# Split fp32r products for three of the six blocks of a down projection

## The chip, the cores and the metric

One core of one Trainium2 chip runs the whole kernel. The metric is the device time in microseconds of one execution, the median of several runs. All times below are of the kernel before the change.

## What is computed

A layer with three residual parts on x of 32 x 32 tokens of 512 numbers (1024 tokens): a cross attention, a gated delta-rule attention, and a mixture of 8 experts, of which each token takes two. The change touches the experts alone:

```python
probs = jax.nn.softmax(scores, axis=-1)
routing_weights, routing_idx = jax.lax.top_k(probs, TOP_K)          # TOP_K = 2 of 8
gate = jnp.einsum('bted,edf->btef', dispatched, gate_proj)           # D = 512, F = 1408
up = jnp.einsum('bted,edf->btef', dispatched, up_proj)
acts = jax.nn.silu(gate) * up
expert_out = jnp.einsum('btef,efd->bted', acts, down_proj)
```

## The kernel before

The kernel sorts the 2 x 1024 token copies by expert into 23 tiles of 128 slots (TILES). The function experts runs them one after the other. A tile's 1408 hidden columns are cut into NB = 6 blocks: five of 256 and one of 128. STEPS = 138 counts the blocks of all tiles, n is the running number, s the tile, b the block in it. Expert weights lie in w_gu (gate and up) and w_d (down); the SP queue loads them for the next tile in three groups each, only where the expert changes (cond=fresh), each group once the last block that used it is done.

Gate and up are computed in "three fp32r products": the activations and the weights are each split into a high part in the narrower type fp32r and a low part (the difference), and hi x hi, hi x lo and lo x hi are added up in PSUM. ScalarE casts the high part of a weight block (gh, L1697), VectorE subtracts to get the low part (gl, L1758), in a ring of four buffers, about three blocks ahead. The activations of a tile are split once (xh L1679, xl L1749).

TensorE's loop does, at each n: gate_up(n) (L1629 to L1631, 12 products), down(n-2) (L1652, two chunks of 128 rows, one for the half block, each an fp32 matmul that the chip runs as two instructions), turn_h(n-1) (L1639, two transposes), and in block 4 turn_x of the next tile (L1616). Between them ScalarE computes silu (L1709), VectorE the product with up (hid, L1791), and ScalarE copies the turned block out of PSUM (hT, L1720).

ScalarE's order at each n is: silu(n), store_y of the tile that ended two blocks ago (L1685 and a DMA from its queue), split_gate_up(n+3), the copy of hT(n-1), and in block 4 take_x. VectorE's is: hid(n), split_gate_up(n+2), in block 4 split_x; once, at n = 24, places() (L1767 to L1773), and in the last blocks gather_sum. GpSimd gathers the rows of y (L1741) once all but the last tile are stored, and VectorE adds them to x_nat (L1778); the last tile's y comes by matmuls (L1673, L1805). Each engine runs its instructions in order, and every hand-over is a semaphore.

Of the kernel before, what the change touches and what calls it, by code (L numbers as in the profile page):

```python
# [11 lines left out]
F32 = mybir.dt.float32  # L12
F32R = mybir.dt.float32r
U8 = mybir.dt.uint8
I32 = mybir.dt.int32
ALU = mybir.AluOpType
# [3 lines left out]
P = 128  # L20
B, N, C = 32, 32, 512
TOK = B * N
NT = TOK // P
# [20 lines left out]
BLK = 256  # L44
RING = 4
NB = -(-F // BLK)
# [1475 lines left out]
def experts(nc, d, ps, ident, x_nat, xn3, slot, slot_f, slot_w, tile_expert, column, hot, scattered, w_gu, w_d, gu_in, d_in, out):  # L1522

    with ExitStack() as ctx:
        sb = lambda name, shape, dt=F32: ctx.enter_context(nc.sbuf_tensor(name, shape, dt))
        sem = lambda name: ctx.enter_context(nc.semaphore(name))
# [2 lines left out]
        gh, gl = ([sb(f"{name}{i}", [P, KC, 2, BLK], F32R) for i in range(RING)] for name in ("gh", "gl"))  # L1532
        silu = [sb(f"silu{i}", [P, BLK]) for i in range(2)]
        hid = [sb(f"hid{i}", [P, BLK]) for i in range(2)]
        hT = [sb(f"hT{i}", [P, BLK // P, P]) for i in range(2)]
        y = [sb(f"y{i}", [P, C]) for i in range(2)]
        yg = [[xn3[:, 2 * (t % (NT // 2)) + r, :] for t in range(NT)] for r in range(2)]
        place, placeT, hot2 = hot, sb("placeT", [P, NT, P]), sb("place2", [P, NT, P])
        rel = sb("rel", [P, 2, NT])
        place_done, p_turned, p_copied, added, f_done, f_added, own = (  # L1540
            sem("place_done"), sem("p_turned"), sem("p_copied"), sem("t_added"), sem("f_done"), sem("f_added"), sem("e_own"))
# [6 lines left out]
        GU_BANK, H_BANK, X_BANK, Y_BANK = 0, 3, 5, 6  # L1548
        STEPS = TILES * NB
# [4 lines left out]
        with nc.Block() as block:  # L1554
# [39 lines left out]
            @block.tensor  # L1594
            def _(pe):
                def pick_first():
                    for k in range(KC):
                        for t in range(NT):
                            mm = pe.matmul(ps[X_BANK][:, k * P:(k + 1) * P], xn3[:, t, k * P:(k + 1) * P], hot[:, t, :],  # L1599
                                           start=(t == 0), stop=(t == NT - 1))  # L1600
                    mm.then_inc(x_turned, 1)

                def turn_places(x):
                    pe.wait_ge(place_done, 1)
                    pe.wait_ge(xl_done, TILES)
                    if x:
                        pe.wait_ge(p_copied, x)
                    for t in range(4):
                        mm = pe.transpose(ps[X_BANK][:, t * P:(t + 1) * P], place[:, 4 * x + t, :], ident[:, :])
                    mm.then_inc(p_turned, 1)  # L1610

                def turn_x(s):
                    pe.wait_ge(x_in[s % 3], 16 * (s // 3 + (s % 3 > 0)))
                    pe.wait_ge(xl_done, s)
                    for k in range(KC):
                        mm = pe.transpose(ps[X_BANK][:, k * P:(k + 1) * P], xs[s % 3][:, k * P:(k + 1) * P], ident[:, :])  # L1616
                    mm.then_inc(x_turned, 1)

                def gate_up(n):
                    s, b, bw = n // NB, n % NB, width(n % NB)  # L1620
                    if b == 0:
                        pe.wait_ge(xl_done, s + 1)
                    pe.wait_ge(gl_done, n + 1)
                    if n >= 3:
                        pe.wait_ge(hid_done, n - 2)
                    bank = ps[GU_BANK + n % 3][:, 0:2 * bw].rearrange("p (a f) -> p a f", a=2)
                    for k in range(KC):
                        hi, lo = gh[n % RING][:, k, :, 0:bw], gl[n % RING][:, k, :, 0:bw]
                        pe.matmul(bank, xh[s % 2][:, k, :], hi, start=(k == 0), stop=False)  # L1629
                        pe.matmul(bank, xh[s % 2][:, k, :], lo, start=False, stop=False)  # L1630
                        mm = pe.matmul(bank, xl[s % 2][:, k, :], hi, start=False, stop=(k == KC - 1))  # L1631
                    mm.then_inc(gu_done, 1)

                def turn_h(n):
                    pe.wait_ge(hid_done, n + 1)
                    if n >= 2:
                        pe.wait_ge(hT_done, n - 1)
                    for c in range(width(n % NB) // P):
                        mm = pe.transpose(ps[H_BANK + n % 2][:, c * P:(c + 1) * P], hid[n % 2][:, c * P:(c + 1) * P], ident[:, :])  # L1639
                    mm.then_inc(h_turned, 1)  # L1640

                def down(n):
                    s, b = n // NB, n % NB
                    pe.wait_ge(hT_done, n + 1)
                    if b % 2 == 0:
                        pe.wait_ge(d_in[b // 2], 16 * (s + 1))
                    if b == 0 and s >= 2:
                        pe.wait_ge(y_ready, s - 1)
                    cs = range(width(b) // P)
                    bank = ps[Y_BANK + s % 2]  # L1650
                    for c in cs:
                        mm = pe.matmul(bank, hT[n % 2][:, c, :], w_d[:, b * (BLK // P) + c, :], start=(b == 0 and c == 0),  # L1652
                                       stop=(b == NB - 1 and c == cs[-1]))
                    mm.then_inc(d_done, 1)

                pick_first()
                for n in range(STEPS + 2):
                    if n < STEPS:
                        gate_up(n)
                    if n >= 2:  # L1660
                        down(n - 2)
                    if 1 <= n <= STEPS:
                        turn_h(n - 1)
                    if n % NB == TURN_AT and n // NB + 1 < TILES:
                        turn_x(n // NB + 1)
                    if n in (STEPS - 4, STEPS - 2):
                        turn_places((n - STEPS + 4) // 2)
                pe.wait_ge(y_ready, TILES)
                pe.wait_ge(p_copied, 2)
                for t in range(NT):  # L1670
                    if t >= 6:
                        pe.wait_ge(f_added, t - 5)
                    pe.matmul(ps[t % 6], placeT[:, t, :], y[(TILES - 1) % 2][:, :], start=True, stop=True).then_inc(f_done, 1)  # L1673

            @block.scalar
            def _(act):
# [14 lines left out]
                def split_gate_up(n):  # L1691
# [3 lines left out]
                    if n >= RING:  # L1695
                        act.wait_ge(gu_done, n - RING + 1)
                    nc.scalar.copy(gh[n % RING][:, :, :, 0:bw].rearrange("p k a f -> p (k a) f"),  # L1697
                                   w_gu[:, :, :, b * BLK:b * BLK + bw].rearrange("p k a f -> p (k a) f")).then_inc(gh_done, 1)

                for n in range(3):  # L1700
                    split_gate_up(n)
                take_x(0)
                for n in range(STEPS + 2):
                    if n < STEPS:
                        bw = width(n % NB)
                        act.wait_ge(gu_done, n + 1)
                        if n >= 2:
                            act.wait_ge(hid_done, n - 1)
                        nc.scalar.activation(silu[n % 2][:, 0:bw], ps[GU_BANK + n % 3][:, 0:bw], ACT.Silu).then_inc(silu_done, 1)  # L1709
                    if n >= 2 and (n - 2) % NB == NB - 1:  # L1710
                        store_y((n - 2) // NB)
                    if n + 3 < STEPS:
                        split_gate_up(n + 3)
                    if 1 <= n <= STEPS:
                        m = n - 1
                        bw = width(m % NB)
                        act.wait_ge(h_turned, m + 1)
                        if m >= 2:
                            act.wait_ge(d_done, m - 1)
                        nc.scalar.copy(hT[m % 2][:, 0:bw // P, :].rearrange("p c n -> p (c n)"),  # L1720
                                       ps[H_BANK + m % 2][:, 0:bw]).then_inc(hT_done, 1)
                    if n % NB == TURN_AT and n // NB + 1 < TILES:
                        take_x(n // NB + 1)
                    if n in (STEPS - 3, STEPS - 1):
                        x = (n - STEPS + 3) // 2
                        act.wait_ge(p_turned, x + 1)
                        nc.scalar.copy(placeT[:, 4 * x:4 * x + 4, :].rearrange("p t n -> p (t n)"), ps[X_BANK]).then_inc(p_copied, 1)
# [18 lines left out]
            def _(dve):  # L1746
# [6 lines left out]
                def split_gate_up(n):  # L1753
                    b, bw = n % NB, width(n % NB)
                    dve.wait_ge(gh_done, n + 1)
                    if n >= RING:
# [3 lines left out]
                                            gh[n % RING][:, :, :, 0:bw].rearrange("p k a f -> p (k a) f").bitcast(F32),  # L1760
                                            ALU.subtract).then_inc(gl_done, 1)

                link = Chain(dve, own).link

                def places():
# [19 lines left out]
                for n in range(STEPS + 1):  # L1785
                    if n < STEPS:
                        bw = width(n % NB)
                        dve.wait_ge(silu_done, n + 1)
                        if n >= 2:
                            dve.wait_ge(h_turned, n - 1)  # L1790
                        nc.vector.tensor_tensor(hid[n % 2][:, 0:bw], silu[n % 2][:, 0:bw], ps[GU_BANK + n % 3][:, bw:2 * bw],  # L1791
                                                ALU.mult).then_inc(hid_done, 1)
                    if 0 < n < STEPS - 2:
                        split_gate_up(n + 2)
                    if n % NB == TURN_AT and n // NB + 1 < TILES:
# [81 lines left out]
```

## Time and profile before

| | |
|---|---|
| median of 3 runs | 1874.05 us (1873.61 to 1875.43) |
| the profiled execution | 1869.62 us, span of the trace 1867.5 us |
| TensorE busy over the span | 1538.5 us (82%) |
| VectorE | 1199.0 us (64%) |
| ScalarE | 713.3 us (38%) |
| the expert stage | from about 1220 us to the end |
| down matmuls L1652 | 506 instructions, 242.2 us busy |
| gh casts L1697, gl subtractions L1758 | 138 each, 242.0 and 290.5 us |

An execution of the kernel is followed by the profiler; the span is from its first to its last instruction. Busy times of TensorE's matmuls overlap each other, so how long a group of them takes is read from the start of one to the start of the next.

### The profile page before, as it was taken

To read this page: it belongs to the slowest core of one execution; us is meant where nothing else is said; L and a number is where in the kernel's file an instruction comes from. 1 tells how busy PE (TensorE), PEld (TensorE's weight loads), DVE (VectorE), ACT (ScalarE), POOL (GpSimd) and SP (SyncE) were. 2 spreads that over 40 slices of the span, in tenths; PEclk is the share of its full clock that TensorE was granted. 3 is DMA by queue.
4 is the path that set the end of the run, shared out by engine and by line. 5 is a ranking of instruction groups with operands and counts; after the bars stand their busy time and mean duration, and the time that the engine had idled before them with its cause. 6 is when DMAs were issued, how large, how long until landed. Compare 5 with 4: busy or idle time off the path is not lost. (4 is left out here: it accounts for less than half of the span.)

```text
span 1867.5 us, 22300 instructions
## 1 busy us (share of the span) xinstructions
PE 1538.5 (82%) x7255; PEld 1144.2 (61%) x7255; DVE 1199.0 (64%) x2644; ACT 713.3 (38%) x1364; POOL 96.1 (5%) x261
## 2 busy tenths in 40 slices
PE   6999999999799999349100089489999999999998
PEld 3888888888667767213000088466666666666664
DVE  4366555665336786999999756455655555556555
ACT  2343343333355455201000222155555555555552
POOL 0000000000000000022112100130000000000003
PEclk9999999999899999779555579689999999999999
DMA  3211011100241441450100231525605514426004
GB/s 119 80 35 33 18 34 34 34 24 10 95 66 44 81 80 41 70 180 1 45 0 0 69 83 36 192 96 209 208 18 203 208 56 165 160 72 207 13 17 141
DMA packets 134201, 152.94 MB, mean 82 GB/s; under 512 B 64096, under 2 KB 84960, under 8 KB 134112
## 3 DMA queue, kind: packets, MB, share of 16 engines
q1 hardware_dynamic: 128384, 137.68, 24.4%
q0 software_dynamic: 2560, 8.39, 1.4%
q10 hardware_dynamic: 3168, 5.77, 0.8%
q8 instruction: 45, 0.74, 0.2%
q14 instruction: 44, 0.36, 0.1%
HBM read 250.25 MB, written 31.33 MB: 151 GB/s over the span
## 5 line engine op out<-in xcount | busy, mean ns | idle before, releaser
L1758 DVE TENSOR_TENSOR gl<-w_gu,gh 128x2048 fp32r<-128x2048 f32 x138 | 290.5, 2106 | 6.8 <-ACT gh L1697 6.7
L1697 ACT CAST gh<-w_gu 128x2048 fp32r<-128x2048 f32 x138 | 242.0, 1755 | 41.8 <-PEq L1413 19.2
L1652 PE MATMUL bank<-w_d,hT 128*128 128x512 f32 x506 | 242.2, 597 | 8.8 <-ACT hT L1720 8.0
L1791 DVE TENSOR_TENSOR hid<-silu,bank 128x256 f32<-128x256 f32 x138 | 55.0, 399 | 264.6 <-ACT silu L1709 264.6
L1629 PE MATMUL bank<-gh,xh 128*128 128x512 f32 (+1 forms) x552 | 217.7, 394 | 1.7 <-DVE xl L1749 1.4
L1631 PE MATMUL bank<-gh,xl 128*128 128x512 f32 (+1 forms) x552 | 205.9, 373 | 0.0
L1630 PE MATMUL bank<-gl,xh 128*128 128x512 f32 (+1 forms) x552 | 205.5, 372 | 0.0
L1229 PE MATMUL bank<-o_v,xnT 128*128 128x64 f32 x256 | 36.1, 310 | 177.9 <-DMA o_v<-scratch_v_rows 177.9
L1229 PEld LDWEIGHTS bank<-o_v,xnT 128*128 128x128 f32 x256 | 35.8, 227 | 178.7 <-DMA o_v<-scratch_v_rows 178.7
L1652 PEld LDWEIGHTS bank<-w_d,hT 128*128 128x128 f32 x506 | 91.7, 189 | 82.0 <-issue 56.9
L1709 ACT ACTIVATE silu<-bank 128x256 f32<-128x256 f32 x138 | 50.6, 367 | 218.3 <-PE bank L1631 216.3
L539 DVE COPY probT<-bank 128x512 f32<-128x512 f32 x64 | 41.1, 683 | 127.9 <-PE bank L421 127.9
L1629 PEld LDWEIGHTS bank<-gh,xh 128*128 128x128 f32 x552 | 104.0, 188 | 22.7 <-issue 6.4
L1631 PEld LDWEIGHTS bank<-gh,xl 128*128 128x128 f32 x552 | 103.8, 188 | 19.3
L1630 PEld LDWEIGHTS bank<-gl,xh 128*128 128x128 f32 x552 | 104.3, 189 | 14.6
L1064 ACT ACTIVATE r_root<-r_nm 128x8 f32<-128x8 f32 x32 | 6.7, 208 | 275.2 <-DVE r_nm L1142 275.2
L1056 PE MATMUL bank<-w_kg,xnT 128*128 128x512 f32 x128 | 60.8, 619 | 52.8 <-DMA bg_row<-in_bg 52.8
L486 ACT ACTIVATE prob<-bank,neg_max 128x257 f32<-128x257 f32 x128 | 59.1, 474 | 74.1 <-DVE neg_max L521 74.1
L1112 DVE TENSOR_TENSOR r_prod<-r_gram,r_pr 128x512 f32<-128x512 f32 (+23 forms) x158 | 83.6, 547 | 0.0
L370 PE MATMUL bank<-xa_wkv_hi,ctx_hi 128*128 128x512 f32 x192 | 78.9, 411 | 0.6 <-PEq L280 0.6
L1056 PEld LDWEIGHTS bank<-w_kg,xnT 128*128 128x128 f32 x128 | 23.6, 195 | 88.4 <-DMA bg_row<-in_bg 53.0
L1639 PEld LDWEIGHTS bank<-ident,hid 128*128 128x128 f32 x253 | 35.4, 140 | 65.9 <-issue 49.8
(296 smaller groups left out, 3097.1 us busy)
## 6 DMA issues: line engine op xcount, KB each, us to landing
w_gu<-in_gate_proj SPq DMA_DIRECT2D x46, 1024.0 KB
w_gu<-in_up_proj SPq DMA_DIRECT2D x46, 1024.0 KB
w_d<-in_down_proj SPq DMA_DIRECT2D x46, 1024.0 KB
w_gu<-in_gate_proj SPq DMA_DIRECT2D x23, 768.0 KB
w_gu<-in_up_proj SPq DMA_DIRECT2D x23, 768.0 KB
w_d<-in_down_proj SPq DMA_DIRECT2D x23, 768.0 KB
ctx_raw<-in_ctxT SPq DMA_DIRECT2D x32, 385.5 KB, 3.7
scratch_x_slots<-r_outw SPq DMA_DIRECT2D x1, 5888.0 KB, 19.3
```

The source lines that it names most:

```text
L370: pe.matmul(bank, hi(k), other_hi(k), start=(k == 0), stop=False)
L486: nc.scalar.activation(prob[s][:, c, :], ps[c][:, 0:M], ACT.Exp, bias=neg_max[s][:, c:c + 1], accum_out=total[s][:, c:c + 1]).then_inc(exp ...
L1056: pe.matmul(ps[n % 8], xnT[:, k, t * P:(t + 1) * P], wg[:, k, hf * 512:(hf + 1) * 512], start=(k == 0), stop=False)
L1112: ins = tt(parts[x][:, a], G[:, :, lo:hi, 2, 0:cols], bc(pr[nxt % 2][:, a, :, None, 0:cols], [SG, hi - lo, cols]), ALU.mult)
L1229: mm = pe.matmul(ps[O_BANK + 2 * s + h // 8][:, (h % 8) * DK:(h % 8 + 1) * DK], outw[s][:, h, :], v_row[s][:, h, :], start=True, stop=True)
L1629: pe.matmul(bank, xh[s % 2][:, k, :], hi, start=(k == 0), stop=False)
L1630: pe.matmul(bank, xh[s % 2][:, k, :], lo, start=False, stop=False)
L1631: mm = pe.matmul(bank, xl[s % 2][:, k, :], hi, start=False, stop=(k == KC - 1))
L1652: mm = pe.matmul(bank, hT[n % 2][:, c, :], w_d[:, b * (BLK // P) + c, :], start=(b == 0 and c == 0), stop=(b == NB - 1 and c == cs[-1]))
L1697: nc.scalar.copy(gh[n % RING][:, :, :, 0:bw].rearrange("p k a f -> p (k a) f"), w_gu[:, :, :, b * BLK:b * BLK + bw].rearrange("p k a f -> ...
L1758: nc.vector.tensor_tensor(gl[n % RING][:, :, :, 0:bw].rearrange("p k a f -> p (k a) f"), w_gu[:, :, :, b * BLK:b * BLK + bw].rearrange("p ...
L1791: nc.vector.tensor_tensor(hid[n % 2][:, 0:bw], silu[n % 2][:, 0:bw], ps[GU_BANK + n % 3][:, bw:2 * bw], ALU.mult).then_inc(hid_done, 1)
```

## The change

In blocks 0, 2 and 4 of each tile down() takes three fp32r products for each chunk, in blocks 1, 3 and 5 it stays with one fp32 matmul. For the changed blocks ScalarE casts dh, the high part of w_d's block, and VectorE subtracts dl; the turned hidden block is copied as fp32r (hh), and VectorE subtracts hl from PSUM. dh, dl, hh and hl are single buffers. On ScalarE the copy of the hidden block moves: in even n it stands behind the gate and up cast and before the new cast, in odd n directly behind silu, ahead of store_y and of the gate and up cast. The buffer place2 gives way to placeT.

```diff
-        hT = [sb(f"hT{i}", [P, BLK // P, P]) for i in range(2)]
+        hh, hl = sb("hh", [P, BLK // P, P], F32R), sb("hl", [P, BLK // P, P], F32R)
+        hT = [hh, sb("hT", [P, BLK // P, P])]
+        dh, dl = sb("dh", [P, BLK // P, C], F32R), sb("dl", [P, BLK // P, C], F32R)
...
                     if n >= 2:
                         pe.wait_ge(hT_done, n - 1)
+                        if n % 2 == 0:
+                            pe.wait_ge(hl_done, n // 2)
...
-                    for c in cs:
-                        mm = pe.matmul(bank, hT[n % 2][:, c, :], w_d[:, b * (BLK // P) + c, :], start=(b == 0 and c == 0),
-                                       stop=(b == NB - 1 and c == cs[-1]))
+                    if b % 2 == 0:
+                        pe.wait_ge(dl_done, n // 2 + 1)
+                        pe.wait_ge(hl_done, n // 2 + 1)
+                        for c in cs:
+                            pe.matmul(bank, hh[:, c, :], dh[:, c, :], start=(b == 0 and c == 0), stop=False)
+                            pe.matmul(bank, hh[:, c, :], dl[:, c, :], start=False, stop=False)
+                            mm = pe.matmul(bank, hl[:, c, :], dh[:, c, :], start=False, stop=False)
+                    else:
+                        for c in cs:
+                            mm = pe.matmul(bank, hT[1][:, c, :], w_d[:, b * (BLK // P) + c, :], start=False,
+                                           stop=(b == NB - 1 and c == cs[-1]))
...
+                def take_hidden(n):
+                    bw = width(n % NB)
+                    act.wait_ge(h_turned, n + 1)
+                    if n >= 2:
+                        act.wait_ge(d_done, n - 1)
+                    nc.scalar.copy(hT[n % 2][:, 0:bw // P, :].rearrange("p c n -> p (c n)"),
+                                   ps[H_BANK + n % 2][:, 0:bw]).then_inc(hT_done, 1)
+
+                def split_down(n):
+                    s, b = n // NB, n % NB
+                    act.wait_ge(d_in[b // 2], 16 * (s + 1))
+                    if n >= 2:
+                        act.wait_ge(d_done, n - 1)
+                    nc.scalar.copy(dh[:, :, :], w_d[:, b * (BLK // P):(b + 1) * (BLK // P), :]).then_inc(dh_done, 1)
...
+                    if n % 2 == 0 and n + 3 < STEPS:
+                        split_gate_up(n + 3)
+                    if 1 <= n <= STEPS:
+                        take_hidden(n - 1)
+                    if n % 2 == 0 and n < STEPS:
+                        split_down(n)
                     if n >= 2 and (n - 2) % NB == NB - 1:
                         store_y((n - 2) // NB)
-                    if n + 3 < STEPS:
+                    if n % 2 and n + 3 < STEPS:
                         split_gate_up(n + 3)
-                    if 1 <= n <= STEPS:
...
+                def split_down(n):
+                    b = n % NB
+                    dve.wait_ge(dh_done, n // 2 + 1)
+                    nc.vector.tensor_tensor(dl[:, :, :], w_d[:, b * (BLK // P):(b + 1) * (BLK // P), :], dh[:, :, :].bitcast(F32),
+                                            ALU.subtract).then_inc(dl_done, 1)
+                    dve.wait_ge(hT_done, n + 1)
+                    nc.vector.tensor_tensor(hl[:, :, :].rearrange("p c n -> p (c n)"), ps[H_BANK][:, 0:BLK],
+                                            hh[:, :, :].rearrange("p c n -> p (c n)").bitcast(F32), ALU.subtract).then_inc(hl_done, 1)
...
+                    if n % 2 and n < STEPS:
+                        split_down(n - 1)
                     if 0 < n < STEPS - 2:
                         split_gate_up(n + 2)
```

## Rows read from the trace of the kernel before

**Rows 1.** Stretch view: us, busy us and count of each engine, PEclk, DMA share, GB/s.

```profile
1224.00:1860.00 636.00, 623.06 (x2573) 424.99 (x2572) 365.41 (x334) 341.44 (x462) 29.58 (x25) 1.00 0.36 125
```

**Rows 2.** Waits of TensorE, 1225 to 1845 us: who waited for whom, total, times, longest.

```profile
PE bank L1652 <- ACT hT L1720: 8.0, 24, 0.4
```

**Rows 3.** Timeline of TensorE: start, duration, instruction, count, idle time before it.

```profile
1293.71 1.98 PE L1652 MATMUL bank<-w_d,hT 128*128 128x512 f32 x4 [0.34 <-ACT hT L1720]
...
1301.14 0.39 PE L1629 MATMUL bank<-gh,xh 128*128 128x512 f32 x1
...
1303.18 1.88 PE L1652 MATMUL bank<-w_d,hT 128*128 128x512 f32 x4
1304.89 0.38 PE L1639 MATMUL bank<-ident,hid 128*128 128x128 f32 x2
...
1305.47 0.36 PE L1629 MATMUL bank<-gh,xh 128*128 128x256 f32 x1
...
1306.98 1.88 PE L1652 MATMUL bank<-w_d,hT 128*128 128x512 f32 x4
1308.69 0.38 PE L1639 MATMUL bank<-ident,hid 128*128 128x128 f32 x2
1308.83 0.48 PE L1629 MATMUL bank<-gh,xh 128*128 128x512 f32 x1
...
1311.65 1.88 PE L1652 MATMUL bank<-w_d,hT 128*128 128x512 f32 x4
...
1320.58 1.98 PE L1652 MATMUL bank<-w_d,hT 128*128 128x512 f32 x4 [0.34 <-ACT hT L1720]
```

**Rows 4.** The same view in the output projection, ahead of the experts.

```profile
1126.05 0.39 PE L1253 MATMUL bank<-wo_hi,o_gT_hi 128*128 128x512 f32 x1
...
1130.83 1.04 PE L1239 MATMUL bank<-ident,r_gram 128*128 128x128 f32 x8
```

**Rows 5.** Timeline of TensorE's weight loads, inside an fp32 down block.

```profile
1303.61 0.19 PEld L1652 LDWEIGHTS bank<-w_d,hT 128*128 128x128 f32 x1 [0.24 <-issue]
```

**Rows 6.** Groups by form: total busy us, mean ns, idle time before them.

```profile
L1697 ACT CAST gh<-w_gu 128x1024 fp32r<-128x1024 f32 x23 | 24.0, 1044 | 0.0
L1758 DVE TENSOR_TENSOR gl<-w_gu,gh 128x1024 fp32r<-128x1024 f32 x23 | 28.0, 1218 | 0.0
```

**Rows 7.** Timeline of ScalarE, columns as in rows 3.

```profile
1273.96 1.91 ACT L1697 CAST gh<-w_gu 128x2048 fp32r<-128x2048 f32 x1 [2.20 <-DMA w_gu<-in_up_proj]
...
1303.38 0.38 ACT L1709 ACTIVATE silu<-bank 128x256 f32<-128x256 f32 x1 [2.23 <-PE bank L1631]
1303.66 1.89 ACT L1697 CAST gh<-w_gu 128x2048 fp32r<-128x2048 f32 x1
1305.45 0.38 ACT L1720 COPY hT<-bank 128x256 f32<-128x256 f32 x1
1305.75 0.59 ACT L1679 CAST xh<-bank 128x512 fp32r<-128x512 f32 x1
```

**Rows 8.** Timeline of VectorE.

```profile
1303.79 0.42 DVE L1791 TENSOR_TENSOR hid<-silu,bank 128x256 f32<-128x256 f32 x1 [3.12 <-ACT silu L1709]
1304.13 2.28 DVE L1758 TENSOR_TENSOR gl<-w_gu,gh 128x2048 fp32r<-128x2048 f32 x1
1306.37 0.69 DVE L1749 TENSOR_TENSOR xl<-bank,xh 128x512 fp32r<-128x512 f32 x1
...
1341.68 0.17 DVE L1767 TENSOR_SCALAR rel<-slot_f 128x16 f32<-128x16 f32 x1
...
1347.26 0.41 DVE L1791 TENSOR_TENSOR hid<-silu,bank 128x256 f32<-128x256 f32 x1
```

**Rows 9.** SP queue's first load of a burst, and the stretch after it (columns of rows 1).

```profile
1265.19 0.40 SPq L1568 DMA_DIRECT2D w_gu<-in_gate_proj  x1
...
1288.00:1290.00 2.00, 2.00 (x9) 1.45 (x8) 0.02 (x2) 0.39 (x1) 0.00 (x0) 1.00 0.06 20
```

**Rows 10.** Timeline of GpSimd: the first gather of y.

```profile
1832.55 0.98 POOL L1741 DMA_INDIRECT xn<-scratch_y_slots,slot  x1 [594.96 <-DMA scratch_y_slots<-y]
```

More of the change, by code:

```diff
@@ L1534, in experts @@
         hid = [sb(f"hid{i}", [P, BLK]) for i in range(2)]
-        hT = [sb(f"hT{i}", [P, BLK // P, P]) for i in range(2)]
+        hh, hl = sb("hh", [P, BLK // P, P], F32R), sb("hl", [P, BLK // P, P], F32R)
+        hT = [hh, sb("hT", [P, BLK // P, P])]
+        dh, dl = sb("dh", [P, BLK // P, C], F32R), sb("dl", [P, BLK // P, C], F32R)
+        hl_done, dh_done, dl_done = sem("hl_done"), sem("dh_done"), sem("dl_done")
         y = [sb(f"y{i}", [P, C]) for i in range(2)]
         yg = [[xn3[:, 2 * (t % (NT // 2)) + r, :] for t in range(NT)] for r in range(2)]
-        place, placeT, hot2 = hot, sb("placeT", [P, NT, P]), sb("place2", [P, NT, P])
+        place, placeT = hot, sb("placeT", [P, NT, P])
+        hot2 = placeT
         rel = sb("rel", [P, 2, NT])
@@ L1709, in _ @@
                         nc.scalar.activation(silu[n % 2][:, 0:bw], ps[GU_BANK + n % 3][:, 0:bw], ACT.Silu).then_inc(silu_done, 1)
+                    if n % 2 == 0 and n + 3 < STEPS:
[4 more added lines that the diff above has]
+                        split_down(n)
                     if n >= 2 and (n - 2) % NB == NB - 1:
                         store_y((n - 2) // NB)
-                    if n + 3 < STEPS:
+                    if n % 2 and n + 3 < STEPS:
                         split_gate_up(n + 3)
-                    if 1 <= n <= STEPS:
[L1715 to L1721, printed above, removed]
                     if n % NB == TURN_AT and n // NB + 1 < TILES:
```

## The prediction

> **What bounds the kernel now.** The page gives means over stages with different limits, so I cut out the expert stage with a stretch view [rows 1]: from 1224 to 1860 us TensorE is busy 623.1 of 636 us at clock 1.00, the weight loads (PEld) 425, VectorE 365, ScalarE 341. TensorE sets the time there, and ScalarE and VectorE have over 40% of theirs free. The waits of TensorE say the same [rows 2]: 8.0 us in 24 waits for hT, a third of a microsecond each, and next to nothing else. Then I read one tile instruction by instruction [rows 3]. A tile has six blocks (0 to 5, the last half as wide), and one turn of TensorE's loop is gate_up(n), down(n-2), turn_h(n-1). The tile's period is 26.87 us, from the hT wait in block 2 at 1293.71 to the one at 1320.58.
>
> **The products themselves.** Busy times on a pipelined TensorE overlap, so I take start to start. The four fp32 matmul instructions of a down block start at 1306.98 and the turn behind them at 1308.69: 1.71 us [rows 3]. Nine fp32r products of 128x512 in gate_up take from 1301.14 to 1303.18, 0.227 us each [rows 3]. The output projection has the same shape of product as the changed one (activations turned and split as weights, 512 columns of a split matrix) in threes of the same order: 21 of them from 1126.05 to 1130.83, 0.228 us [rows 4]. A changed block has two chunks of three products: 6 x 0.227 = 1.36 us. Gain 0.35 us a block. There are 3 x 23 = 69 such blocks; the end of the kernel hangs on the store of tile 21 (below), before which 66 have run: 66 x 0.35 = **23.1 us**. Bounds: 0.43 a block, 28 us, if a product went at half of an fp32 instruction (1.71 / 4 / 2 = 0.214); and 0.25, 16 us, if each group also paid the 0.10 us that an fp32 group pays behind a wait (1.98 for four against 1.88). I take the pace between them, since gate_up and the projection both show it.
>
> The fp32 rows leave the weight loader 0.24 us idle before a load of 0.19 us [rows 5]; at 0.227 us a product such a load still fits beside the product ahead. The Trainium skill (TensorE: Matmul & The Clock Gate, Back-to-back issue gap) gives N/2.4 + 2.5 ns warm, 216 ns for 512 columns; by it the six products would take 1.30 us and the sum would gain some 4 us more. The rows of this case show 227 ns, and they decide.
>
> **The order on ScalarE.** Now hT is copied behind the cast of gate and up (gh), which in block 1 starts late because the store of y goes first. That is TensorE's 0.33 us wait in each tile [rows 2, 3]. The change puts take_hidden right behind silu in odd steps, the store of y and the gh cast behind it. hT of block 0 then comes as soon as it is turned, over 2 us ahead of its use. 23 of the 24 waits go (the last lies behind the store of tile 21): 23 x 0.33 = **7.7 us**. Bound: nothing, if hl, which now ends that chain, is just as late.
>
> **What is added elsewhere.** Per changed block ScalarE casts dh 128x1024, 1.04 us like the half gh, VectorE subtracts dl 128x1024, 1.22 us like the half gl [rows 6], and hl from PSUM, 128x256, 0.42 us like hid [rows 8]. Per tile that is 3.1 us on ScalarE and 4.9 on VectorE. Start to start (each overlaps the next a little) VectorE's tile is 5 gl x 2.24, one 1.18, hid 1.9, xl 0.65, dl 3.5, hl 1.0: 19.5 us, in a new period of 26.87 - 0.33 - 3 x 0.35 = 25.5. ScalarE has about 17.6. Both fit on average; whether they fit in their order has to be walked.
>
> The walk counts from the end of gate_up(4) on TensorE, with latencies of the rows: silu starts 0.2 behind the end and hid 0.61 (1303.18, 1303.38, 1303.79), gh follows silu 0.28 later and takes 1.79, hT 0.30, xh 0.60, hid to gl 0.34 [rows 3, 7, 8]; a whole gate_up is 2.82, the half one 1.51, turn_h 0.14, with turn_x 0.58 [rows 3]; hT starts 0.42 behind the turn's start (estimate: the turn's 0.38 and a hand-over). ScalarE: silu 0.2, gh to 2.3, hT(3) to 2.6, dh(4) to 3.5, xh to 4.1. TensorE: down(2) 1.36, turns 0.58, gate_up(5) 1.51, end at 3.45; down(3) in fp32 1.71, turn 0.14, so gate_up(0) of the next tile may start at 5.3. It needs xl: VectorE has it at 4.8. Margin 0.5. silu(5) is 0.4 late behind xh, hid(5) is done at 5.0, dl(4) at 6.2, hl(4) at 6.5, gl(1) at 8.8. gate_up(0) ends at 8.1 and down(4) needs hl(4) there: margin 1.6. down(4) and the short turn end at 9.5, where gate_up(1) needs gl(1): margin 0.7. hid(0) 9.1, gl(2) 11.3; gate_up(1) ends at 12.3; hid(1), dl(0), hl(0) to 14.8, needed at 16.15: margin 1.3; gl(3) at 17.1, needed at 17.65: margin 0.6. An ordinary odd step has 1.7 for hl and 1.0 for gl. So there is no wait in the steady tile, though three margins are only 0.5 to 0.7. The wait that turn_h gains (hl_done) is for hl of two blocks before, long past. What queues behind a waiting hl on VectorE is gl of three blocks ahead, and it is in the walk.
>
> **Where the cover is gone.** (a) places(), once, in block 0 of tile 4, holds VectorE from 1341.68 to 1347.26, 5.6 us [rows 8]. In the walk that moves hl(0) to 18.8 against 16.15 and gl(3) to 21.1 against 17.65: **+3.4 us** (bounds 1 to 5.6). (b) The first tile starts with an empty pipe, and the same count puts hl(0), then gl(3), behind: **+0.7** (estimate from the same rows; 0 to 2). (c) Where the expert changes (7 times by ScalarE's waits for w_gu), gh waits for the load: 2.20 us at 1273.96 [rows 7], 8.8 us from its issue [rows 9]. By the walk gh(0) is 0.7 to 1.4 us late and xh with it, so gate_up(0) waits up to 0.3: **+1** for all seven (0 to 5). The dh cast needs w_d two blocks earlier than the matmul did. The burst of loads issued from 1265.19 has ended by 1288 [rows 9], and dh(0), carried over to the new clock, comes at 1285.6; w_d's first part is not the burst's last, so I take nothing. (d) The tail. The gathers on GpSimd start when the y of tile 21 has landed (1832.55) [rows 10], and they, the sums and the last additions make the end; TensorE's last blocks lie beside that path. The y copy now has take_hidden ahead of it: +0.5. The gathers wait for VectorE's sums, which in the last tile stand behind dl and hl: +0.3. Together **+0.8**. w_d's loads keep their place in the SP queue; GpSimd's queue and the stages before 1224 us are untouched.
>
> **Sum.** -23.1 - 7.7 + 3.4 + 0.7 + 1.0 + 0.8 = -24.9 us. The profiled execution took 1869.62 us (span 1867.5), so 1844.7 for a like one. The median of the runs is 1874.05, 4.4 above it: **1849**.
>
> **Rivals.**
> 1. A thin margin fails in each tile: the three places of 0.5 to 0.7 us are late by 0.5 us a tile in all, 22 x 0.5 = 11, so 1860. For it: the walk is good to 0.1 or 0.2 us a step only, and it has many. Against: gl takes the same 2.28 with a gh at its side (1304.13) as any other [rows 7, 8], so the engines don't slow each other. 0.13.
> 2. Slower: VectorE's line sets the period. hl(4), blocked on hT(4), keeps gl(1), and TensorE waits at every start of a tile. It decides once the stretch of 8.8 us up to gl(1) grows past 9.5; to eat the whole 25 us and 8 more, 1.5 a tile, it must grow to 11.0, by a quarter, for instance by hT coming a step later than I read. Then 1849 + 22 x 1.5 = 1882. Against it are the equal durations just named. 0.06.
> 3. The products' gain doesn't come: six weight loads replace four, and if the two more were exposed they would cost 2 x 0.19 = 0.38 us a block against the 0.35 gained. Only the hT waits go, less the small terms: 1849 + 66 x 0.38 = 1874, no change. Trace Analysis of the Trainium skill (Identifying the Most-Contended Engine) judges TensorE's headroom by the busy share of its weight loads, which this change raises. Here that share is 67% [rows 1]; 69 x 2 loads of 0.19 more, 26 us, leave it under 75%, so by itself the rule doesn't bind. The rows at 0.227 speak against exposed loads. 0.06.
> 4. The hT waits stay, as hl waits: 1857. It lies within the range. 0.06.
>
> **How the numbers follow.** The forecast holds 0.69; its own range is 1842 (all 69 blocks, and no price for a, b and c) to 1854 (b and c at their upper bounds). With rivals 4 and 1 the range is 1842 to 1862. Under 1842 I leave 0.06 in the forecast's share, over 1862 some 0.12. A measurement of this kernel tells about 0.2% (3.7 us) from no change. Faster by more than that: 0.87; within it: 0.06 (rival 3); slower: 0.07 (rival 2 and a rest).
>
> **What would show it.** After: six products of a changed block start to start in 1.36 us; a tile period of 25.5 us and no TensorE wait for hT in block 2; ScalarE near 66% and VectorE near 76% busy in a plain stretch; one gap of some 3 us behind places(), for hl and gl; y of tile 21 some 25 us earlier, and the stretch from it to the end unchanged within 1 us. Waits for xl or gl once a tile would be rival 1, a period over 26.9 rival 2, 1.7 us for six products rival 3. What would make me wrong most simply is an engine's order that I walked wrongly at the turn from one tile to the next.

## The result and the profile after

The changed kernel takes 1846.45 us (median of 4, 1845.26 to 1846.84) against 1873.98 in the same session: ratio 0.9842, 95% interval 0.9824 to 0.9861 (the quotient of the two medians is 0.9853, inside it). Forecast were 1849, in 1842 to 1862. Its profiled execution took 1845.26 us (span 1843.2), so profile against profile it is 24.4 us shorter, where the sum said 24.9.

The busy line of the profile's page (engine, busy us, share of the span, instructions) and the stretch view for two whole tiles (columns of [rows 1]):

```profile
PE 1516.0 (82%) x7393; PEld 1175.5 (64%) x7393; DVE 1300.7 (71%) x2782; ACT 778.1 (42%) x1433; POOL 97.1 (5%) x261
```

```profile
1436.94:1462.15 25.21, 25.21 (x117) 19.32 (x116) 19.40 (x20) 17.48 (x24) 0.00 (x0) 1.00 0.46 163
1462.15:1487.36 25.21, 25.21 (x118) 19.32 (x117) 19.75 (x20) 17.93 (x24) 0.00 (x0) 1.00 0.64 223
```

In a plain tile TensorE is busy all the time at clock 1.00, VectorE 77 to 78%, ScalarE 69 to 71% and the weight loads 77%. TensorE's timeline (columns of [rows 3]), a changed block, the turn of tiles, and one place where the expert changes:

```profile
1303.09 0.39 PE L1662 MATMUL bank<-dh,hh 128*128 128x512 f32 x1
...
1304.45 0.38 PE L1646 MATMUL bank<-ident,hid 128*128 128x128 f32 x2
...
1308.39 0.48 PE L1634 MATMUL bank<-gh,xh 128*128 128x512 f32 x1
...
1312.60 0.47 PE L1634 MATMUL bank<-gh,xh 128*128 128x512 f32 x1
...
1320.79 0.47 PE L1634 MATMUL bank<-gh,xh 128*128 128x512 f32 x1
...
1332.18 1.99 PE L1667 MATMUL bank<-w_d,hT 128*128 128x512 f32 x4 [0.28 <-ACT hT L1720]
...
1436.94 0.60 PE L1621 MATMUL bank<-ident,xs 128*128 128x128 f32 x4
1462.15 0.60 PE L1621 MATMUL bank<-ident,xs 128*128 128x128 f32 x4
```

Six products take from 1303.09 to 1304.45, 1.36 us, where four fp32 instructions took 1.71 [rows 3]. The turn of x at 1436.94 and at 1462.15 gives the period: 25.21 us, where it was 26.87. Of the 21 periods between the first and the last turn of x, 17 are 25.21 within 0.01; the others are taken up below. TensorE's waits, 1220 to 1860 us (who waited for whom, total, times, longest):

```profile
PE bank L1688 <- DVE x_nat L1844: 5.1, 1, 5.1
PE bank L1662 <- DVE hl L1797: 3.7, 2, 2.7
PE bank L1667 <- ACT hT L1720: 1.8, 5, 0.6
...
PE bank L1634 <- DVE gl L1786: 0.3, 1, 0.3
```

The 8.0 us in 24 waits for hT [rows 2] are now 1.8 in 5. Of the two waits for hl one, 2.7 us, lies behind places(); the other, 1.0, in the last tile, beside the path that ends the kernel, as does one of the five for hT (0.35).

The wait behind places() cost more than itself. TensorE around it, and the stretch view of three pieces of it (the number behind POOL is the granted clock):

```profile
1342.47 0.48 PE L1634 MATMUL bank<-gh,xh 128*128 128x512 f32 x1
...
1348.20 0.47 PE L1662 MATMUL bank<-dh,hh 128*128 128x512 f32 x1 [2.73 <-DVE hl L1797]
...
1350.31 0.80 PE L1634 MATMUL bank<-gh,xh 128*128 128x512 f32 x1
...
1354.36 1.88 PE L1667 MATMUL bank<-w_d,hT 128*128 128x512 f32 x4
```

```profile
1348.00:1349.00 1.00, 0.80 (x4) 0.69 (x5) 1.00 (x2) 0.00 (x0) 0.00 (x0) 1.00 0.67 256
1351.00:1352.00 1.00, 1.00 (x4) 0.81 (x3) 1.00 (x1) 0.80 (x1) 0.00 (x0) 0.50 0.03 8
1353.00:1354.00 1.00, 1.00 (x6) 0.83 (x5) 0.00 (x0) 0.00 (x0) 0.00 (x0) 1.00 0.00 0
```

From 1342.47 to 1354.36 are 11.89 us; the same instructions one tile earlier took 7.18 (1316.44 to 1323.62), so 4.7 us are lost. The down block starts 2.9 late, and gate_up(3) at 1350.31 starts 3.5 late, 0.06 behind the end of the gl(3) that it needs (1350.25). The last 1.2 us are lost behind that, since the granted clock had fallen from 1.00 to 0.50 (2.4 to 1.2 GHz): from 1349.43 to 1352.61 products go at about 0.43 us instead of 0.227. In the kernel before, where TensorE waited 0.28 us at this place, the clock stayed at 1.00.

VectorE around the same turn of tiles:

```profile
1307.20 0.69 DVE L1777 TENSOR_TENSOR xl<-bank,xh 128x512 fp32r<-128x512 f32 x1 [0.87 <-ACT xh L1694]
...
1309.47 2.28 DVE L1786 TENSOR_TENSOR gl<-w_gu,gh 128x2048 fp32r<-128x2048 f32 x1
...
1317.87 2.28 DVE L1786 TENSOR_TENSOR gl<-w_gu,gh 128x2048 fp32r<-128x2048 f32 x1
```

xl is ready at 1307.89 and gate_up(0) starts at 1308.39: margin 0.5, as walked. gl(1) ends at 1311.75, 0.85 before 1312.60 (walked 0.7). gl(3) ends at 1320.15, 0.64 before 1320.79 (walked 0.6).

Where the 24.4 us lie, from the two profiled executions (starts of the first matmul behind the routing, of the first and the last gather of y, and the span's end):

| stretch | before | after | difference | by the sum |
|---|---|---|---|---|
| up to the first matmul of the experts | 1220.57 | 1223.14 | +2.6 | 0 |
| to the first gather of y [rows 10] | 611.98 | 583.58 | -28.4 | -25.2 |
| first to last gather | 21.62 | 23.07 | +1.5 | +0.3 |
| to the end | 13.33 | 13.41 | +0.1 | 0 |

So the total agrees better than its parts, and that is luck: the expert stage gained 3.2 us more than forecast, the tail lost 1.2 more, and 2.6 came in ahead of everything that was changed. That last part is no effect of the change: in another execution of the same changed kernel (below) the experts start at 1220.58.

### The profile page after: what moved, and what is told of

Same layout as the page of the kernel before. It is cut to its first block and busy times, and to the rows that moved or that the text cites. A ratio compares the mean times of both kernels' runs of the same rounds, so it can differ in the third digit from the quotient of the medians.

```text
span 1843.2 us, 22920 instructions
## 1 busy us (share of the span) xinstructions
PE 1516.0 (82%) x7393; PEld 1175.5 (64%) x7393; DVE 1300.7 (71%) x2782; ACT 778.1 (42%) x1433; POOL 97.1 (5%) x261
## 3 DMA queue, kind: packets, MB, share of 16 engines
q1 hardware_dynamic: 128384, 137.68, 24.4%
## 5 line engine op out<-in xcount | busy, mean ns | idle before, releaser
L1635 PEld LDWEIGHTS bank<-gl,xh 128*128 128x128 f32 x552 | 104.6, 189 | 14.6
L1667 PE MATMUL bank<-w_d,hT 128*128 128x512 f32 x230 | 110.4, 594 | 1.8 <-ACT hT L1720 1.8
L1794 DVE TENSOR_TENSOR dl<-w_d,dh 128x1024 fp32r<-128x1024 f32 x69 | 84.0, 1218 | 0.0
L481 ACT COPY xkT<-bank 128x512 f32<-128x512 f32 x64 | 37.6, 588 | 91.3 <-PE bank L372 91.3
```

The costliest lines, as they stand in the source:

```text
L1667: mm = pe.matmul(bank, hT[1][:, c, :], w_d[:, b * (BLK // P) + c, :], start=False, stop=(b == NB - 1 and c == cs[-1]))
L1794: nc.vector.tensor_tensor(dl[:, :, :], w_d[:, b * (BLK // P):(b + 1) * (BLK // P), :], dh[:, :, :].bitcast(F32), ALU.subtract).then_inc(dl ...
```

## Experiments

The sessions of the experiments had the kernel before at 1877.2 and 1877.5 us (1872.3 to 1884.4), a scatter of several us. Medians are therefore read by their ratio to the kernel before of their session, and small terms from the trace: the period of a plain tile (from turn to turn of x) and the stretch from the first matmul of the experts to the first gather. A ratio is compared with the changed kernel's 0.9842; 0.001 of it is 1.9 us. Two profiles of the changed kernel have 583.58 and 585.49 us for that stretch (the second waits 1.3 us longer for hT where the expert changes), so differences under 2 us in it say nothing alone; the waits then count. The kernel before has one profile only. Some diffs show only the main lines of an edit.

**1. Only the order.** The kernel before with ScalarE's copy of hT moved:

```diff
-                    if n >= 2 and (n - 2) % NB == NB - 1:
-                        store_y((n - 2) // NB)
-                    if n + 3 < STEPS:
+                    if n % 2 == 0 and n + 3 < STEPS:
                         split_gate_up(n + 3)
                     if 1 <= n <= STEPS:
                         m = n - 1
...
+                    if n >= 2 and (n - 2) % NB == NB - 1:
+                        store_y((n - 2) // NB)
+                    if n % 2 and n + 3 < STEPS:
+                        split_gate_up(n + 3)
```

> The kernel before with only ScalarE's order changed: the copy of the turned block stands ahead of store_y and of the gate and up cast in odd n, all products stay fp32. Theory A (a wait that the trace shows as 0.33 us of idle costs 0.60 us start to start, since the product ahead overlaps it and the group restarts cold): 23 waits x 0.60 less some 1 to 2 us of new waits where the expert changes, so about 1862. Theory B (the idle column is the whole cost): 23 x 0.33 less the same, about 1868.

Measured: 1860.01 us, ratio 0.9906 (0.9889 to 0.9922). TensorE's timeline and waits:

```profile
1439.25 0.60 PE L1616 MATMUL bank<-ident,xs 128*128 128x128 f32 x4
1465.51 0.60 PE L1616 MATMUL bank<-ident,xs 128*128 128x128 f32 x4
```

```profile
PE bank L1629 <- DVE gl L1760: 0.9, 1, 0.9
PE bank L1652 <- ACT hT L1718: 0.8, 2, 0.5
```

The period is 26.26 us: one wait that the idle column gives as 0.33 us was worth 26.87 - 26.26 = 0.61. Over 23 tiles that is 14 us; with the new waits and the later store of y the stretch to the first gather is 600.94 against 611.98, 11.0 less. By the ratio the kernel gained 17.6 us (14.6 to 20.8), where A had 12 and B (7.7 less the same) 6. Theory A holds, if anything too low; B does not.

**2. The products in the old order.**

```diff
+                    if n >= 2 and (n - 2) % NB == NB - 1:
+                        store_y((n - 2) // NB)
-                    if n % 2 == 0 and n + 3 < STEPS:
+                    if n + 3 < STEPS:
                         split_gate_up(n + 3)
                     if 1 <= n <= STEPS:
                         take_hidden(n - 1)
                     if n % 2 == 0 and n < STEPS:
                         split_down(n)
-                    if n >= 2 and (n - 2) % NB == NB - 1:
-                        store_y((n - 2) // NB)
-                    if n % 2 and n + 3 < STEPS:
-                        split_gate_up(n + 3)
```

> The changed kernel with ScalarE's old order: store_y, gate and up cast, then the copy of the turned block. Theory A (the order is a condition of the change): hl of block 0 comes about 1.1 us after TensorE needs it and gl of block 3 behind it about 0.7 us late, so about 40 us more than the changed kernel, 1880 to 1890, slower than before. Theory B (the order and the products are separate gains): only the old hT waits come back, 1846 + 14 = 1860.

Measured: 1878.53 us, ratio 1.0009 (0.9996 to 1.0022): no change clear of noise to the kernel before. Waits of TensorE, 1225 to 1845 us:

```profile
PE bank L1662 <- DVE hl L1795: 23.6, 26, 2.5
PE bank L1634 <- DVE gl L1784: 5.8, 22, 0.3
```

A wait for hl and then one for gl in each tile, as walked. The usual period is 26.87 us (12 of the 21 lie within 0.02 of it, the others above), 1.66 over the changed kernel's and the same as the kernel before's. To the first gather it is 31.9 us more than the changed kernel (615.47 against 583.58), by the ratios 31: short of A's 40, and twice B's 14. The order gains by itself too (experiment 1), but without it the products gain nothing: it is a condition of theirs.

**3. All splits made, no products.**

```diff
-                            pe.matmul(bank, hh[:, c, :], dh[:, c, :], start=(b == 0 and c == 0), stop=False)
-                            pe.matmul(bank, hh[:, c, :], dl[:, c, :], start=False, stop=False)
-                            mm = pe.matmul(bank, hl[:, c, :], dh[:, c, :], start=False, stop=False)
+                            mm = pe.matmul(bank, hh[:, c, :].bitcast(F32), w_d[:, b * (BLK // P) + c, :], start=(b == 0 and c == 0), stop=False)
```

> The changed kernel with all splits made and waited for, but the down blocks 0, 2 and 4 as one fp32 matmul a chunk on the rounded hidden values (the low part of the hidden values is left out of the result). Theory A (a block gains 0.35 us, the splits cost TensorE nothing in the steady tile): 66 x 0.35 = 23 above the changed kernel, 1869 to 1870. Theory B (the prediction's extra 3 us came from the products, 0.40 us a block): 1873. If the splits cost something in the steady tile, this kernel less the first one of this call is more than 8 us.

Measured: 1865.2 us, ratio 0.9931 (0.9906 to 0.9955). Against the changed kernel's 0.9842 that is 17 us by the ratios and 604.47 - 583.58 = 20.9 by the stretch (19.0 to the second profile), both under A's 23.

```profile
1444.40 0.60 PE L1621 MATMUL bank<-ident,xs 128*128 128x128 f32 x4
1470.65 0.60 PE L1621 MATMUL bank<-ident,xs 128*128 128x128 f32 x4
```

The period is 26.25 us. To experiment 1 that is 0.01: 8 us a tile of added work on ScalarE and VectorE cost TensorE nothing. To the changed kernel it is 1.04, three times 0.35. So a block gains what was forecast, and B's 0.40 is out. That the 20.9 are 2.2 us under the 66 x 0.35 fits the tiles in which the expert changes: by the periods the changed kernel loses 3.5 us there, this one 1.4. That the loads come later against a shorter tile is likely, but was not tried.

**4. 1.2 us more on VectorE, at two places.** dl of block 4 made twice, and in another kernel dl of block 2 (b == 2 in the line below):

```diff
                     dve.wait_ge(dh_done, n // 2 + 1)
+                    if b == 4:
+                        link(nc.vector.tensor_tensor(dl[:, :, :], w_d[:, b * (BLK // P):(b + 1) * (BLK // P), :], dh[:, :, :].bitcast(F32),
+                                                     ALU.subtract))
```

> The changed kernel with VectorE's subtraction for dl of block 4 done twice, 1.2 us more in each tile, where the walk leaves 0.7 to 0.85 us until gl(1) is needed. Theory A (the margin by the walk decides): 0.3 to 0.6 us a tile, 1853 to 1860. Theory B (VectorE's free quarter of the tile takes it up): 1846 to 1847.

> The same 1.2 us of extra VectorE work a tile, but for dl of block 2, where hl has 1.7 us until it is needed. Theory A (the place decides, not the amount): no change to the changed kernel, 1846 to 1847. Theory B (VectorE's total decides): the same cost as with block 4.

Measured: block 4 1858.89 us, ratio 0.9904 (0.9879 to 0.9929); block 2 1843.74 us, 0.9823 (0.9803 to 0.9843). Waits of TensorE, first with block 4, then with block 2:

```profile
PE bank L1634 <- DVE gl L1786: 6.2, 23, 0.4
PE bank L1662 <- DVE hl L1800: 4.8, 2, 3.2
```

```profile
PE bank L1662 <- DVE hl L1800: 3.8, 2, 2.8
PE bank L1667 <- ACT hT L1720: 3.1, 5, 1.3
```

The same work, 1.2 us a tile, costs 0.47 us a tile in the one place (period 25.68, from 1444.89 to 1470.57) and nothing in the other (25.21, from 1437.30 to 1462.51). VectorE is busy 81% of the first period and 82% of the second. The shift exceeds the margin by 1.2 less 0.85, that is 0.35; the rest is about what the restart of the group costs.

**5. The remaining waits.** places() cut into five parts in block 3 of tiles 4 to 8; the first gate and up load of the next tile issued ahead of the last down load of this one; and both, with the last eight matmuls in eight PSUM banks:

```diff
-                    if n == 4 * NB:
-                        places()
+                    if n % NB == 3 and 4 <= n // NB < 9:
+                        places(n // NB - 4)
```

```diff
                     load_down(s, e, 1, fresh)
+                    e2, fresh2 = expert(s + 1)
+                    load_x(s + 2)
+                    load_gate_up(s + 1, e2, 0, fresh2)
                     load_down(s, e, 2, fresh)
```

```diff
-                    if t >= 6:
-                        pe.wait_ge(f_added, t - 5)
-                    pe.matmul(ps[t % 6], placeT[:, t, :], ...)
+                    pe.matmul(ps[t], placeT[:, t, :], ...)
```

> The changed kernel with places() cut into five parts, in block 3 of tiles 4 to 8, where VectorE waits for silu. Theory A (its 2.7 us wait for hl and the restart are lost for good): 3 us less than the changed kernel, 1843.5. Theory B (TensorE catches it up later): no change.

> The changed kernel with the first gate and up load of the next tile issued ahead of the last down load of this one, some 3.7 us earlier. Theory A (the five waits for hT in block 5 where the expert changes come from the late load, 0.36 + 0.26 us each): 3 us less, 1843.5. Theory B (they come from ScalarE's fuller queue): no change. If w_d's last part comes late now, slower.

> Both of these, and the last eight matmuls into eight PSUM banks, so that none waits for VectorE. In the changed kernel the last one waits 5.1 us and then runs at clock 0.50, but VectorE's seven additions hide all but 0.3 us of it. Theory A: 3 + 3 + 0.4, so 1840. Theory B (the end hangs on the gathers alone, whose pace sets it, and gains before the store of tile 21 don't reach it in full): 1843 or more.

Measured: 1843.01 us (0.9818, 0.9801 to 0.9836), 1841.31 us (0.9812, 0.9791 to 0.9832), 1839.89 us (0.9799, 0.9778 to 0.982). The intervals overlap each other, and the first two that of the changed kernel, so the single steps are read from the trace; the third lies just under it. The stretch to the first gather is 581.15, 579.54 and 575.29 us, that is 2.4, 4.0 and 8.3 less than the changed kernel's 583.58. Waits of TensorE with places() spread, then with the early load, then together:

```profile
PE bank L1667 <- ACT hT L1720: 3.0, 5, 1.3
PE bank L1662 <- DVE hl L1797: 1.0, 1, 1.0
```

```profile
PE bank L1671 <- DVE hl L1806: 3.5, 2, 2.5
...
PE bank L1676 <- ACT hT L1729: 0.4, 1, 0.4
```

```profile
PE bank L1671 <- DVE hl L1804: 1.0, 1, 1.0
...
PE bank L1676 <- ACT hT L1727: 0.4, 1, 0.4
```

Each step takes away the waits that it was meant for: hl's 2.7 us at places(), and hT's where the expert changes (the 0.4 that stays is the one in the last tile). By the waits theory A of each holds. What they are worth is read from the periods. With both steps all 21 are 25.21 within 0.01; the changed kernel loses 8.2 us in four of them: 4.7 to places() and 3.5 where the expert changes (in each of the four; places() falls into one of them). With the early load alone the tile of places() still loses 4.3, and with places() spread the clock stays at 1.00 there. So places() costs 4 to 5 us and not the 3 of the expectation; the first step shows only 2.4 of it in the stretch, in part since this execution waits 2.7 us for hT where the expert changes, against 1.5 in the changed kernel. What the eight banks give was not measured by itself.

**6. The tail.** The last tile's down blocks in fp32, without dh, dl and hl, which TensorE's idle end can afford; the changed kernel again beside it; and everything together:

```diff
-                    if n % 2 and n < STEPS:
+                    if n % 2 and n < STEPS - NB:
                         split_down(n - 1)
```

> The changed kernel itself once more, so that the next two are compared with it in one session: 0.984 of the kernel before, as measured.

> The changed kernel with the last tile's down blocks all in fp32 and without its dh, dl and hl, since TensorE's last blocks lie beside the path that ends the kernel. Theory A (the 16 gathers of y take 23.1 us instead of 21.6 because VectorE's dl and hl run beside them): the stretch from the first to the last gather falls to 21.6, the time by 1.5 us. Theory B (the gathers' pace has another cause): no change within 0.3 us of that stretch.

> places() spread, the load ahead, eight banks and the last tile in fp32 together. Theory A of each: 8.3 us less than the changed kernel for the first three by the stretch up to the first gather, and 1.5 more at the end, so about 9 to 10 below it, 0.979 of the kernel before. If the last tile gives nothing: 8 below.

The diff is the line for VectorE; ScalarE and TensorE have the like. Measured in one session: the changed kernel 1845.04 us (0.9843, 0.982 to 0.9865), with the last tile in fp32 1843.61 (0.9831, 0.9809 to 0.9853), everything together 1835.64 (0.9784, 0.9763 to 0.9806). GpSimd's gathers (start, duration) in the changed kernel, VectorE beside them, and the gathers with the last tile in fp32:

```profile
1806.72 0.98 POOL L1769 DMA_INDIRECT xn<-scratch_y_slots,slot  x1 [566.55 <-DMA scratch_y_slots<-y]
1808.01 2.00 POOL L1769 DMA_INDIRECT xn<-scratch_y_slots,slot  x1 [0.31 <-issue]
...
1811.56 1.77 POOL L1769 DMA_INDIRECT xn<-scratch_y_slots,slot  x1 [0.30 <-issue]
1813.64 1.62 POOL L1769 DMA_INDIRECT xn<-scratch_y_slots,slot  x1 [0.30 <-issue]
...
1829.79 1.07 POOL L1769 DMA_INDIRECT xn<-scratch_y_slots,slot  x1 [0.30 <-issue]
```

```profile
1806.89 2.28 DVE L1786 TENSOR_TENSOR gl<-w_gu,gh 128x2048 fp32r<-128x2048 f32 x1
...
1811.30 1.22 DVE L1794 TENSOR_TENSOR dl<-w_d,dh 128x1024 fp32r<-128x1024 f32 x1
...
1813.23 1.22 DVE L1786 TENSOR_TENSOR gl<-w_gu,gh 128x1024 fp32r<-128x1024 f32 x1
```

```profile
1803.70 0.98 POOL L1770 DMA_INDIRECT xn<-scratch_y_slots,slot  x1 [566.09 <-DMA scratch_y_slots<-y]
...
1808.53 0.94 POOL L1770 DMA_INDIRECT xn<-scratch_y_slots,slot  x1 [0.30 <-issue]
1809.77 0.94 POOL L1770 DMA_INDIRECT xn<-scratch_y_slots,slot  x1 [0.30 <-issue]
...
1825.76 0.95 POOL L1770 DMA_INDIRECT xn<-scratch_y_slots,slot  x1 [0.30 <-issue]
```

With the last tile in fp32 the gathers take from 1803.70 to 1825.76, 22.06 us, of which GpSimd waits 1.4 for VectorE's sums (0.3 before). The changed kernel has 23.07, and 23.48 in its second profile. The fourth and fifth gather take 0.94 each there instead of 1.77 and 1.62: those are the ones beside which VectorE ran dl (1811.30) and the gl behind it (1813.23). For these two gathers theory A holds. For the stretch as a whole it is not shown: experiment 3 and the second kernel of experiment 4 keep dl and hl in the last tile, and their gathers take 21.91 and 22.14 us; the others with them take 22.8 to 23.8. What decides is which of VectorE's instructions a gather happens to meet (last section). The median's 1.4 us lies within the scatter. Everything together lies clearly below the changed kernel, as forecast (0.979).

## Why the prediction was right, point by point

- **TensorE bounds, the products gain 0.35 us a block.** Right: 1.71 became 1.36, and experiment 3 isolates 1.04 us a tile. The start-to-start pace of gate_up and of the output projection carried over exactly. The Trainium skill's 216 ns a product (TensorE: Matmul & The Clock Gate, Back-to-back issue gap) would have been 1.30 for six; the trace has 0.227 us a product here too, and decides.
- **The hT waits.** The mechanism was right and the term mis-sized: 23 x 0.33 = 7.7 us was taken from the idle column, and each wait was worth 0.61 (experiment 1, and the period's 1.66 less 3 x 0.35), 14 us. The idle column counts from the modelled end of the product ahead, 0.39 us from its start, while an unhindered next one starts 0.23 behind it; and a group of four that starts behind a wait takes 0.1 us longer, which I had read as 1.98 against 1.88 and used only as a bound elsewhere. The forecast period of 25.5 was 0.28 too long for this reason. It makes the steady tiles worth 4.1 us more than forecast: 21 periods between the first and the last turn of x, 1.66 each, are 34.9, where the two terms add up to 30.8. Against it stand places() and the changes of expert, 2.1 us dearer than forecast (below); the pieces ahead of the first and behind the last turn, 46.0 us before and after, came out 1.2 us better. That gives the stage's extra 3.2.
- **The walk.** Right: no wait in the steady tile, and the three thin margins 0.5, 0.85 and 0.64 for 0.5, 0.7 and 0.6. Experiment 4 shows that the margin decides and not VectorE's share. Rivals 1 and 2 did not happen. With the old order of ScalarE the waits of rival 2 did come, and the period was the 26.87 of the kernel before.
- **places(), +3.4.** The mechanism came as walked: hl, then gl(3), put gate_up(3) 3.5 us late. Behind it the fallen clock, which the prediction had not, took 1.2 more. Of these 4.7 us the kernel before had lost 0.55 at the same place, so the change cost 4.1.
- **Changes of expert, +1.** The term was too small and the place wrong: I had the late gh delay xh and gate_up(0); it delays hT of block 3, since silu and a further gh cast stand ahead of it on ScalarE. It does so in four tiles, 1.5 us of idle and 3.5 by their periods (the second profile of the changed kernel: five waits, 3.1 us of idle), of which the kernel before had lost 1.2 already: 2.4 for a term of 1. ScalarE waits for w_gu seven times, as before, but three of these waits did not reach TensorE.
- **The tail, +0.8.** The gathers themselves slowed by 1.5 us, which no step of mine had (last section); the wait for VectorE's sums, 0.3 us, is as long as before, so that term was nothing. The stretch behind the store of tile 21, forecast as unchanged within 1 us, grew by 1.5.
- **Rival 3** is refuted by the period; **rival 4** too, since no wait stands in block 2.
- **From the profile to the median** I carried 4.4 us, the distance of the profiled execution of before from its median. After, it was 1.2. That is 3.2 us of pure scatter of one execution, and the whole distance from 1849 to 1846.45 is smaller. So the forecast was right by its mechanism, and close to the microsecond by luck.
- **Shares.** VectorE came as said (76%). ScalarE at 66% was a slip: the walk's own 17.6 us of 25.5 are 69%, and 69 to 71% were measured.

## What to carry to other kernels

A mean busy share does not say whether an engine can take more work: walk the in-order queues from one hand-over to the next and look for the smallest margin; 1.2 us of work cost nothing in one place and 0.47 us a tile in another. Work that feeds the bounding engine must also stand in the right order in its queue: here the faster products gave nothing at all until the copy moved ahead of the casts. And take a stall of TensorE as the difference of start-to-start times with and without it, not as the idle column: here 0.61 against 0.33 us. After a longer stop look at the granted clock too: a wait of 2.7 us cost 4.7.

## What the runs showed of the hardware

**GpSimd's gathers wait out a VectorE instruction with two SBUF inputs.** A gather takes 0.94 to 0.98 us when no such instruction (gl, dl, or a sum of gathered rows) is under way as it starts. Otherwise it takes what is left of that instruction and about 0.82 us more. The gather at 1808.01 finds 1.16 us of gl left and takes 2.00, the one at 1811.56 finds 0.96 of dl left and takes 1.77, the one at 1813.64 finds 0.81 of gl left and takes 1.62; one that finds 0.1 or less left shows no delay. An instruction of VectorE that starts within the gather does not lengthen it: gl at 1806.89 leaves the first one at 0.98. Over the 13 traces of this case 202 of the 208 gathers are within 0.04 us of this; the other six started at most 0.07 us behind one of VectorE's sums and still took 0.95. The kernel before had such gathers too (2.22 and 1.68 us), so the change only moved and added encounters. Which part of a gather is held up was not tried. The Trainium skill (SBUF — State Buffer, Who interferes with whom) says that a VectorE instruction with two SBUF inputs contends with a GpSimd instruction that reads SBUF; these durations agree with it.

**A faster TensorE can meet a slower clock.** The wait behind places() above is one case. The tail is the other: TensorE now stands idle for 5.1 us before its last two matmuls, which wait for VectorE. The stretch view before and during them, and the matmuls:

```profile
1832.00:1834.00 2.00, 0.00 (x0) 0.00 (x0) 0.93 (x2) 0.00 (x0) 0.00 (x0) 1.00 0.29 104
1834.00:1836.00 2.00, 0.01 (x1) 0.02 (x1) 1.93 (x4) 0.00 (x0) 0.00 (x0) 0.54 0.00 0
1836.00:1838.00 2.00, 2.00 (x3) 0.97 (x4) 2.00 (x4) 0.00 (x0) 0.00 (x0) 0.50 0.60 223
```

```profile
1835.98 3.78 PE L1688 MATMUL bank<-y,placeT 128*128 128x512 f32 x4 [5.12 <-DVE x_nat L1844]
```

The granted clock falls from 1.00 to 0.50 (2.4 to 1.2 GHz) after TensorE stood idle, and four instructions take 3.78 us; before the change the wait was 2.08 us, the clock stayed at 1.00 and the same four took 1.98. VectorE's additions hide all but 0.29 us of it. At places() nothing hides it, and 1.2 us went.
